# Graph transformer layers on one core: POOL waits for the near products ahead of a part's 13th gather

## The reference, cut to what matters

```python
def _L1_gnn_ref(x, W, attn_src, attn_dst, edge_index, edge_type):
    h_all = jnp.einsum('nf,rof->rno', x, W).reshape(r, n, h, d)      # one table row per relation and node
    src, dst = (edge_index[0], edge_index[1])
    h_src = h_all[edge_type, src]
    h_dst = h_all[edge_type, dst]
    scores = jnp.einsum('ehd,hd->eh', h_src, attn_src) + jnp.einsum('ehd,hd->eh', h_dst, attn_dst)
    scores = jnp.where(scores > 0, scores, NEG_SLOPE * scores)
    amax = jnp.maximum(jax.ops.segment_max(scores, dst, num_segments=n), 0.0)
    w = jnp.exp(scores - amax[dst])
    denom = jax.ops.segment_sum(w, dst, num_segments=n) + 1e-12
    msg = h_src * (w / denom[dst])[..., None]
    out = jax.ops.segment_sum(msg, dst, num_segments=n)
```

## Time and profile before

| What | Value |
|---|---|
| Median of 3 runs | 4776.59 us (4770.77 to 4787.19) |
| The profiled execution's own time | 4744.46 us |
| Its span, first to last instruction | 4742.8 us |
| Mean granted TensorE clock in it | 0.818 |
| Busy in the span | PE 70%, PEld 51%, DVE 44%, POOL 23%, ACT 13% |
| Indirect transfers of the ring (L1972) | 784, 780.0 us of POOL |

### The profile page before, as it was taken

One profiled execution on the slowest core, in us unless ns is written; L12 is line 12 of the kernel. 1 busy time (PEld: TensorE's weight loads), 2 busy tenths in 40 slices (PEclk: granted clock), 3 DMA queues, 4 the chain that ended last, 5 costly groups with the idle time before them and its releaser, 6 DMA issues. The chain is left out here.

```text
span 4742.8 us, 52284 instructions
## 1 busy us (share of the span) xinstructions
PE 3298.2 (70%) x14322; PEld 2412.2 (51%) x14323; DVE 2080.1 (44%) x4400; ACT 620.1 (13%) x1234; POOL 1075.0 (23%) x1246
## 2 busy tenths in 40 slices
PE   1899799679846317999549603267777777737998
PEld 0666588568725215777424303144555554525555
DVE  6999601310143630000132284366666666742333
ACT  0111100110022102232102100000000000002222
POOL 2300100000010231000310001666666666400000
PEclk9999899889978658999769856577777776757999
DMA  3522244234300012112223102344444444200000
GB/s 102 218 95 95 100 125 125 69 116 133 97 10 0 0 55 77 49 53 82 62 90 145 62 0 43 102 113 120 119 123 120 120 120 119 71 31 20 14 13 27
DMA packets 311385, 383.64 MB, mean 81 GB/s; under 512 B 42672, under 2 KB 255489, under 8 KB 307841
## 3 DMA queue, kind: packets, MB, share of 16 engines
q1 hardware_dynamic: 240642, 221.16, 14.3%
q0 software_dynamic: 49040, 140.22, 10.3%
q10 hardware_dynamic: 21616, 21.21, 1.5%
HBM read 270.97 MB, written 111.53 MB: 81 GB/s over the span
## 5 line engine op out<-in xcount | busy, mean ns | idle before, releaser
L1972 POOL DMA_INDIRECT att_ring<-relation_rows,table_row x784 | 780.0, 995 | 441.1 <-issue 221.8
L2083 PE MATMUL att_acc<-att_ring,att_onehot 128*128 128x264 f32 x1568 | 529.5, 466 | 214.0 <-issue 196.6
L2083 PEld LDWEIGHTS att_acc<-att_ring,att_onehot 128*128 128x128 f32 x1568 | 340.4, 227 | 353.4 <-issue 302.4
L446 PE MATMUL counts_acc<-onehot_lo,onehot_key 128*128 128x400 bf16 x2000 | 361.7, 336 | 44.6 <-DVE onehot_key L428 44.6
L425 DVE TENSOR_SCALAR onehot_lo<-node_ids,source_lo 128x800 bf16<-128x800 int16 x1000 | 350.9, 419 | 0.0
L446 PEld LDWEIGHTS counts_acc<-onehot_lo,onehot_key 128*128 128x128 bf16 x2000 | 267.8, 139 | 142.6 <-DVE onehot_key L428 84.3
L625 PE MATMUL agg_agg<-x_gnn,agg_slab 128*128 128x257 f32 x1250 | 278.6, 382 | 66.1 <-DMA agg_slab<-edge_counts 66.1
L2046 PE MATMUL att_po<-att_near,att_onehotT 128*128 128x64 f32 x1568 | 229.9, 305 | 94.8 <-DVE att_onehotT L2143 51.8
L625 PE MATMUL agg_agg<-xn,agg_slab 128*128 128x257 f32 x1250 | 277.5, 381 | 22.3 <-DMA agg_slab<-edge_counts 22.3
L625 PEld LDWEIGHTS agg_agg<-x_gnn,agg_slab 128*128 128x128 f32 x1250 | 238.6, 191 | 102.3 <-DMA agg_slab<-edge_counts 66.5
L2046 PEld LDWEIGHTS att_po<-att_near,att_onehotT 128*128 128x128 f32 x1568 | 216.5, 219 | 103.9 <-issue 103.0
(11 more groups left out here) (391 smaller groups left out, 4355.0 us busy)
## 6 DMA issues: line engine op xcount, KB each, us to landing
agg_slab<-edge_counts SPq DMA_DIRECT2D x50, 1600.0 KB, 7.4
edge_counts<-counts_out SPq DMA_DIRECT2D x100, 400.0 KB, 2.4
relation_rows<-tab_out SPq DMA_DIRECT2D x25, 1056.0 KB, 4.0
att_targets<-targets SPq DMA_DIRECT2D x28, 896.0 KB
wide_w<-L_ffn_W ACTq DMA_DIRECT2D x14, 1024.0 KB, 6.9
att_ring<-relation_rows,table_row POOLq DMA_INDIRECT x784
expert_rows_in<-blank_rows POOLq DMA_DIRECT2D x34, 256.0 KB
expert_rows_out<-blank_rows POOLq DMA_DIRECT2D x33, 256.0 KB
```

Source lines behind the costliest of these rows:

```text
L446: mm = nc.tensor.matmul(acc[:, k, h, 0:HALF_LO], oh_key[:, k, :, j], oh_lo[:, k, j, h * HALF_LO:(h + 1) * HALF_LO], start=False, stop=Fals ...
L1972: nc.gpsimd.indirect_dma_start(slots(p)[:, j, :], None, rows_of, bass.IndirectOffsetOnAxis(ap=c.row[:, n:n + 1], axis=0)).then_inc(landed[ ...
L2083: mm = nc.tensor.matmul(acc[:, 0:RW], oh[:, j, :], slots(p)[:, j, :], start=j == 0, stop=False)
```

## The change

One wait more on POOL. From part 3 on, ahead of the transfer with index 12 of a part (its 13th, the first of group 3), behind the wait on `used` that is there already, POOL waits until `own_sum` has reached p, which is when all near products of part p-1 are done. Nothing else changes.

```diff
                     if j % MGRP == 0 and p >= RING:
                         pl.wait_ge(used, (p - RING) * MG + j // MGRP + 1)
+                    if j == 3 * MGRP and p >= RING:
+                        pl.wait_ge(own_sum, p)
                     nc.gpsimd.indirect_dma_start(slots(p)[:, j, :], None, rows_of,
                                                  bass.IndirectOffsetOnAxis(ap=c.row[:, n:n + 1], axis=0)
                                                  ).then_inc(landed[p % RING], 16)
```

## The result

The changed kernel takes 4807.12 us (median of 5 runs, 4804.22 to 4834.31), the kernel before 4776.59 us (5 runs, 4770.77 to 4787.19): ratio 1.0071, 95% interval 1.004 to 1.0103. It is slower by 30.5 us, where 78 were forecast. The profiled execution took 4804.22 us (span 4802.5), 59.8 more than the one before. That one, at 4744.46 us, lies 26 us under the fastest of the five runs of before. The whole difference between the two profiled executions is in the attention stage: from its first gather to its last instruction it takes 1282.7 us for 1220.9, and the rest of the program 3519.8 for 3521.9.

The account below looks back on a forecast made before the run. Bound: a loop of waits in the attention stage, PE's signals late while gathers stream. 24 x (44.5 - 41.05) = +83, -10, +5 gives +78: 4822 from the profiled 4744.5, plus 32 makes 4855 us; range 4737 to 4890, own range 4829 to 4890.

Parts of the forecast that it names:

- the hinge: Attention stage: PE's signals fall behind while gathers stream, up to 15 us, and catch up when they pause; how much overlap matters.
- the sign: What would show the forecast right on POOL: one stop a part, ahead of the 13th transfer, of 7 us or more.
- The faster case: Rival: only the dense near products suffer from gathers, so the period is POOL's 39.8 us, total 4739; chance 0.32.
- no tie between transfers and PE: Rival: near products' signal is late for a reason gathers don't touch; nothing moves, 4777 us; chance 0.08.
- the period: Time from one part to the next in the attention stage: 44.5 us for 41.05, over 24 periods +83 us.
- the first signal's gain: Start of the waiting parts: the first near products' signal comes 8 transfers earlier, 8 x 1.25 = -10 us.
- the end's loss: End of the stage: DVE stands 5 us behind the signal where it stood beside it, +5 us.
- the offset: Median of the runs shown, 4776.6, lies 32 us above the profiled execution, 4744.5; added to 4822 to forecast 4855.
- The forecast's lower end: Lower end of the forecast's own range: a period of 43 us gives +52, total 4829 us.
- the restart behind the signal: POOL's loop: after the near products' signal POOL restarts its transfers 0.3 us later.
- the store: PE under gathers: gets through 40 pairs plus one per 1.41 us of a run's age; refilled only by a pause.
- the stop that I priced at nothing: POOL stopping also at a part's first transfer because message group 0 is late; counted as costing nothing.

Follow-up runs that it names:

- f3_dup8: Kernel before with near group 1 of each part from part 2 on computed twice (8 pairs more on PE a turn), late chip: 4804.62 us, ratio 1.0126.
- f4_drain: Kernel before with two more POOL stops a part, ahead of the 9th and 21st transfer, until its own transfers landed, late chip: 4738.92 us, ratio 0.9986.
- f1: The changed kernel again, on a chip with late answers, against the kernel before at 4745.06 us: 4798.83 us, ratio 1.0109.
- h1_change: The changed kernel on a chip with prompt answers, against the kernel before at 4589.87 us: 4590.28 us, ratio 1.0001.
- f2_plain: The kernel before, unchanged, profiled on the late chip where its runs took 4745.06 us: 4742.27 us, stage 1220.83 us.

## Why the prediction was right in sign and wrong in size

**Right.** On the late chips the hinge holds: signals of PE fall behind while gathers stream, and those that wait come through when the gathers stop. f3_dup8 and f4_drain act on it from both sides, and the change moves POOL's stops, not anybody's work. POOL stops ahead of the 13th transfer in every part (2.7 to 10.0 us, 5.1 in the mean, where 7 or more was the sign), never ahead of the 21st; the mask's wait is 0.03 us for 7.04. The faster case (39.8 a part) fell: the traces of the changed kernel have 43.5 and 44.6 a part in the mean, and so did the case of no tie between transfers and PE.

**Wrong: the sum, 78 forecast and 30.5 measured.** Two terms carry the miss of 48 us.

The first is the period. From the first gather, the masks of parts 2 and 26 and the end of the stage come at 159.4, 1142.9 and 1220.9 us before, at 153.3, 1197.8 and 1282.7 after. So the first signal's gain was 6 us where 10 stood, the end's loss 7 where 5 stood, and the 24 periods between gave 1044.5 - 983.5 = +61 where 24 x (44.5 - 41.05) = +83 stood: 43.5 each in the mean, 1.0 less than taken. Together +62 for +78. The turn shown has 44.4, and the mean of f1's profiled run is 44.6. But the periods of the changed kernel aren't regular: its masks come 34.7 to 48.2 us apart, and the sum took one pattern for all 24.

The second is the offset. The forecast added 32 us, the distance of the median of before from its profiled execution, to a sum made against that execution. Behind the change it is 2.9 (4807.12 less 4804.22). That is 29 of the 48 us; the period and the two small terms make 16 of the rest, and outside the stage the program is 2 us shorter. Nothing had shown that these 32 us would stay; the kernel before took 4740 to 4747 in 15 runs on the chip of f1, so they are no property of its program. Why the five runs of before took 4771 to 4787 us, where the profiled execution took 4744, stays open, and with it how much of the measured 30.5 belongs to the change: the two profiled executions are 59.8 apart, the medians on the chip of f1 54.

The forecast's lower end was also added up wrongly. By its own terms a period of 43 gives 24 x 1.95 - 10 + 5 = +42, 4819, where +52 and 4829 stood. And the restart behind the signal, 0.3 in the sum, took 0.8 in all 25 parts of the changed kernel (3451.46 to 3452.24 in the turn shown).

**Wrong on the way: the store.** A store that only pairs empty and age refills allowed 54 pairs at age 20. In the turn shown, counted as the prediction counts (from 1.6 us behind POOL's restart), the row was late at 27 pairs and age 17, the column at 36 pairs and age 20. But 27 pairs at age 10 were answered at once (the flip back at 3447.93). Before, 45 pairs at age 8 were 1.7 us late. So age does not give. Nor does a short stop refill it whole: in the changed kernel a row transpose through at 3302.60, 13 pairs behind a stop of 1.34 us, was answered 4.5 us late, at 3307.14. And f3_dup8 has both cases side by side: behind the stop of 7.44 us the flip back, at 53 pairs and age 9, was 6.1 us late; behind the stop of 5.24 us the column transpose, at 66 pairs and age 15, was answered in 0.04 us. Neither pairs nor age nor the transfers since the last stop sort these cases, so the store is no model of what happens. It missed that the first column, not the second, was the late answer. And the stop that I priced at nothing, ahead of a part's first groups, for message groups 0 to 2, takes 62 us in parts 4 to 26; held signals come through in it. One stop of 8 us was forecast, two of 2.6 and 5.7 came in the turn shown; the period is near the forecast by that accident.

**Missed altogether: the chip.** All of it was argued from one trace as if the lateness were the kernel's. On four of the five chips that followed there is none, and the kernel takes 4589 us, bound by POOL's transfers; the change, measured on one of the four, is worth 0. The case "no tie between transfers and PE", given 0.08, is what holds there, and its 36.4 us of transfers are the period. The Trainium skill's rule in "SBUF — State Buffer", section "Who interferes with whom", that "DMA never contends with a compute engine", agrees with the traces of those four chips. On the late ones the gathers do hold up what waits for PE; the rule is about SBUF's ports, and no run here shows where the two meet.

**Open.** What delays PE's signals, whether pairs, busy time or bytes count, and what sets a late chip apart from a prompt one (the chip itself, or what else runs beside). On each of the five chips the runs of the kernel before lie within 0.3%, so there it doesn't change from run to run. Whether the product itself or only its signal is late can't be told either: the trace records the signal (at 3150.14 for the near products of the earlier trace rows), but the ends of matmuls in it are modelled. And but for the change itself, no edit was run on more than one late chip.

## What to carry to other kernels

Where a signal is answered long after its work is through, find what ends the wait, and time the same kernel on another chip before pricing a change by it: a wait may cost 1% on one and nothing on the next. A wait added to one queue saves nothing by itself; see what the pauses that it replaces did for the others. And a sum from a profiled execution is to be set against that execution; carry its offset to the median with its own doubt.

## What the runs showed of the hardware

- One and the same kernel takes 4589 us on four chips, 4745 on another, and took 4777 in the runs that the forecast was made for. The difference between the first two lies in the stage with indirect transfers: 1068 us in h1_change for 1221 in f2_plain, with 3519 and 3520 us for the rest of the program. (The kernel before has no trace on a prompt chip; the changed one takes the same time there.)
- On the late chips PE's signals come up to 15 us late under indirect transfers (22 in the opening), PE goes down to a pair each 1.4 us, later 2.8, and the held signal comes 3.3 to 3.5 us after POOL stops ahead of index 20 of the kernel before, 2.4 us in the turn shown of the changed one. On the prompt ones the same pairs under the same transfers (133 GB/s, more than the 119 of the earlier trace rows) are answered in 0.04 us. So it isn't the traffic's rate alone.
- 28 indirect transfers of 128 rows take 36.6 us of POOL when nothing stops them; with rows of half the length 36.3.
